# Gated delta rule plus mixture of experts on one core: decay exponents made on GpSimd instead of TensorE, and a reordered VectorE and GpSimd programme

## The chip, the cores and the metric

One core of a Trainium2 chip (trn2). The metric is the device time of one execution in microseconds. Engine names follow the profile: PE is TensorE, DVE is VectorE, ACT is ScalarE, POOL is GpSimd, SP is SyncE, whose queue here only issues DMAs.

## The reference, cut to what matters

```python
# x: (2, 2048, 256), 16 heads of 64
q, k, v = causal_dwconv(x @ Wq.T), causal_dwconv(x @ Wk.T), causal_dwconv(x @ Wv.T)   # 4 taps and a bias
g, beta = log_sigmoid(x @ Wg.T), sigmoid(x @ Wb.T)
k = k / clip(norm(k), 1e-12);  q = q * 64 ** -0.5
# per head, over time:
#   S = exp(g_t) * S + beta_t * (k_t v_t^T - k_t (S^T k_t)^T);   o_t = S^T q_t
x = layernorm(x + o @ Wo.T)
x = layernorm(x + shared_expert(x) + top6_of_64_experts(x))
```

## The kernel before, in words

The kernel has three phases. `gates_phase` computes the gates and, for all chunks of 64 tokens, the running sums of g inside a chunk. It stores these sums as rows in DRAM (`g_rows`) and their exponentials in `eg_rows`. `delta_phase` runs the recurrence in chunks. `ffn_phase` is the output projection, the layer norms and the experts; the change does not touch it.

`delta_phase` works on 64 macros. A macro is 256 tokens of both batches for one pair of heads, that is 16 units of 64 tokens in a 128x512 layout: 8 blocks of 64 columns (C = 64), and 64 partitions for each of two halves. A loop over `SLOTS` = 71 slots is written out for every engine, and each engine runs its own list of steps in order, tied to the others by semaphores. In slot t the macro m = t is projected (`project`, three outputs k, v, q through the single PSUM bank `p_j`), the macro `before` = t - 1 goes through keys, values, Gram products and mask, the macro `mi` = t - 5 has its triangular inverse completed (`inverse_r` to `horner`), and two steps of the state chain run (`chain_step`, called `one` and `two_`). Every second slot starts a group of two macros whose 16x16 diagonal blocks are inverted by forward substitution in 15 rows (`substitute`, L628 and L631, two small DVE operations per row on the tiles `xi`, `kb` and `outer`).

A causal convolution of four taps is done in this way: ACT writes the last tap with the bias (`last_tap`), DVE adds taps 2, 1 and 0 with `scalar_tensor_tensor` (`conv`, L574) for k and q. For v it adds taps 2 and 1 (`conv_values`, L588), and PE the rest.

The decay matrix of a macro, exp(cum_query - cum_key) with the later keys masked, is made in `exponents` (L417): one fp32 matmul over 82 partitions in which selector rows pick the row of sums and subtract the other, into `p_j`. ACT takes the exponential out of `p_j` into `ex` (`decay`, L730). POOL multiplies it by beta over the key length (`weight`, L876), and DVE uses it in `mask` (L617), which is nearly the last DVE step of a slot. The operands of that matmul are `arg_l` and `arg_r`: constants loaded once, and the rows of the macro loaded from `g_rows` by three small DMAs (`load_rows`, L269 and L271).

Other names: `residual` L646, `gate` L598 (keys and queries times `eg`), `update` L654, `lengths` L605, `inverse_lengths` L609, `horner` L638 on DVE; `decay_state` L888, `off_diagonal` L858, `carry_in` L844, `carry_out` L851, the copy of the identity into `xi` L908, `clip` L863, `factors` L869 and L870, `roots` L882 (a power of 128x8 elements) on POOL. The SP queue in a slot: `load_blocks` L299, `load_rows`, `load_decays` L279, `load_weights` L288, `load_inverse` L316 and L321, `store_o` L330, `store_inverse` L307.

Which operands lie in PSUM matters below. `residual`, `update`, `horner` and `mask` read one operand from PSUM (`p_c`, `p_i`, `p_xy`). `conv`, `conv_values`, `gate` and both operations of `substitute` read two tensors from SBUF.

Of the kernel before, what the change touches and what calls it, by code (L numbers as in the profile page):

```python
# [7 lines left out]
ALU = mybir.AluOpType  # L8
# [26 lines left out]
C_ID, C_INCL, C_SUF, C_ONES, C_SAME, C_SWAP, C_OFF, C_EYE, C_STRICT, C_REST, C_END = (  # L35
    0, 128, 256, 384, 512, 640, 768, 832, 1088, 1216, 1344)
# [16 lines left out]
def gates_phase(nc, a, s):  # L53

    sem = s.sem
    with ExitStack() as own:
# [15 lines left out]
        rows_out, cleared, args_in = sem("g_rows_out"), sem("g_cleared"), sem("g_args_in")  # L72
# [6 lines left out]
        def _(sp):  # L79
# [6 lines left out]
            for i in range(2):  # L86
                sp.dma_start(s.arg_l[i][:, :], a["arg_l"]).then_inc(args_in, 16)
                sp.dma_start(s.arg_r[i][:, :], a["arg_r"]).then_inc(args_in, 16)
            sp.wait_ge(args_in, 64)
# [23 lines left out]
        def _(pe):  # L113
# [19 lines left out]
            for k in range(4):  # L133
                pe.transpose(p_row[:, k * 128:k * 128 + 128], za[:, k * 128:k * 128 + 128],
                             s.const[:, C_ID:C_ID + 128]).then_inc(sums, 1)

        @block.vector
        def _(ve):
# [12 lines left out]
            ve.tensor_copy(za[:, 0:512], p_cum[:, :]).then_inc(dve, 1)  # L151
# [36 lines left out]
def delta_phase(nc, a, s):  # L188
# [5 lines left out]
    with ExitStack() as own:  # L194
# [15 lines left out]
        eg, ex, arg_l, arg_r = two("eg", 520), s.ex, s.arg_l, s.arg_r  # L210
# [51 lines left out]
        def _(sp):  # L262
            def load_rows(m):

                e = m % 2
                if m >= 2:
                    sp.wait_ge(exped, m - 1)
                for sh in range(2):
                    sp.dma_start(view(arg_l[e], sh * C, (1, C), parts=(64 + sh * 8, 8)),  # L269
                                 bass.AP(s.g_rows, m * 1024 + sh * 512, [[C, 8], [1, C]])).then_inc(r_in[e], 16)  # L270
                sp.dma_start(view(arg_r[e], 0, (1, 512), parts=(80, 2)),  # L271
                             bass.AP(s.g_rows, m * 1024, [[512, 2], [1, 512]])).then_inc(r_in[e], 16)
# [61 lines left out]
            load_tokens(0)  # L334
            load_weights(1)
# [23 lines left out]
        def _(pe):  # L359
            def project(m, n, done):  # L360
                e = m % 2
                if n == 1 and m == 0:
                    pe.wait_ge(tap_k, 1)
                if n == 1 and m >= 1:
                    pe.wait_ge(exped, m)
# [156 lines left out]
            for t in range(SLOTS):  # L522
# [13 lines left out]
                if is_macro(before):  # L536
                    exponents(before)
                if is_macro(before):
# [23 lines left out]
        def _(ve):  # L562
            def conv(m, i, tapped, done, taps=(2, 1, 0)):
# [3 lines left out]
                for tap in taps:  # L567
# [9 lines left out]
            def conv_values(m):  # L577
# [3 lines left out]
                for tap in (2, 1):  # L581
                    if tap == 2:
                        ve.wait_ge(tap_v, m + 1)
                        ve.wait_ge(carried, m + 1)
                    else:
                        ve.wait_ge(conv_v, 2 * m + 1)
                    column = (m % NPAIR * 3 + 2) * (TAPS + 1) + tap
# [984 lines left out]
```

## Time and profile before

| | |
|---|---|
| median of 3 runs | 1839.95 us (1837.96 to 1852.81) |
| the profiled execution | 1854.48 us, its span 1852.7 us |
| busy in the span | PE 1576.1, DVE 1201.7, ACT 890.0, POOL 863.5 us |
| slots of the delta phase | from about 60 to about 1200 us |

Times in the rows are microseconds from the span's start. The profiled execution is 0.8% above the median, so a difference worked out from the profile is added to the median.

### The profile page before, as it was taken

What the parts mean: (1) busy time and instruction counts of PE and PEld (TensorE: products, weight loads), DVE (VectorE), ACT (ScalarE), POOL (GpSimd) and SP (SyncE); (2) the same over time, 40 slices, a digit from 0 to 9 for tenths busy, and PEclk for the clock granted to TensorE, in tenths of its full rate; (3) what the DMA queues carried; (4) which work ended last, traced back from release to release, by engine and by line L of the source; (5) the groups of instructions that cost most, each with busy time, mean ns of one, the idle gap of its engine ahead of it and who ended that gap; (6) DMA issues with size and microseconds to landing.
All of it is one profiled execution on the core that took longest, in us unless ns stands there. A gap on an engine that the chain in (4) does not pass through costs nothing. (4 is left out here: it accounts for less than half of the span.)

```text
span 1852.7 us, 73957 instructions
## 1 busy us (share of the span) xinstructions
PE 1576.1 (85%) x31244; PEld 1175.0 (63%) x31244; DVE 1201.7 (65%) x3061; ACT 890.0 (48%) x2282; POOL 863.5 (47%) x1070
## 2 busy tenths in 40 slices
PE   7478999999899999999999997667888985898990
PEld 6235666666666666666666665556777874787870
DVE  1388988888889889888888886234445553222224
ACT  1276767767767767667667664100011110133333
POOL 0034444443444444434444443116655665577775
PEclk9799999999999999999999998887889997999995
DMA  6235564565555655655656554274444420499757
GB/s 269 82 83 115 114 133 114 124 128 116 123 126 114 138 113 123 135 114 113 137 114 126 111 117 99 56 240 118 140 130 133 138 80 27 110 259 248 166 88 284
DMA packets 521402, 245.45 MB, mean 132 GB/s; under 512 B 423888, under 2 KB 485968, under 8 KB 520176
## 3 DMA queue, kind: packets, MB, share of 16 engines
q1 hardware_dynamic: 368976, 200.72, 41.2%
q10 hardware_dynamic: 133632, 20.98, 6.1%
q0 software_dynamic: 18464, 19.03, 5.8%
q8 instruction: 247, 4.05, 0.9%
q14 instruction: 83, 0.68, 0.1%
HBM read 169.29 MB, written 71.37 MB: 130 GB/s over the span
## 5 line engine op out<-in xcount | busy, mean ns | idle before, releaser
L375 PE MATMUL delta_p_j<-delta_xt,delta_w 128*128 128x512 f32 x768 | 387.7, 628 | 30.5 <-DMA delta_xt<-in_xt 17.5
L574 DVE SCALAR_TENSOR_TENSOR delta_kq<-delta_hist,cw,delta_kq 128x512 f32<-128x512 f32 x384 | 298.6, 778 | 30.7 <-ACT delta_kq L722 23.7
L1395 POOL DMA_INDIRECT slot_tokens<-mix_tokens,mix_slot x192 | 188.5, 982 | 115.5 <-DVE mix_slot L1266 59.8
L715 ACT ACTIVATE delta_hist<-delta_p_j 128x512 f32<-128x512 f32 x192 | 114.8, 598 | 240.6 <-PE delta_p_j L375 233.4
L375 PEld LDWEIGHTS delta_p_j<-delta_xt,delta_w 128*128 128x128 f32 x768 | 132.0, 192 | 146.3 <-issue 111.8
L888 POOL TENSOR_TENSOR delta_sd<-state,eg_end 128x256 f32<-128x256 f32 x128 | 104.4, 816 | 258.2 <-DVE state L654 258.2
L1074 PE MATMUL mix_p_y<-mix_wo,mix_ot 128*128 128x256 f32 x512 | 134.3, 407 | 33.3 <-issue 15.6
L863 POOL TENSOR_SCALAR delta_n<-delta_n 128x8 f32<-128x8 f32 x64 | 15.5, 242 | 287.3 <-DVE delta_n L605 287.3
L1165 PE MATMUL mix_p_h<-mix_wo,w 128*88 128x128 f32 x1024 | 126.2, 277 | 13.5 <-ACT mix_wo L1351 10.4
L588 DVE SCALAR_TENSOR_TENSOR delta_yv<-delta_hist,cw,delta_yv 128x512 f32<-128x512 f32 x128 | 132.1, 1032 | 8.2 <-ACT delta_yv L722 5.9
L1074 PEld LDWEIGHTS mix_p_y<-mix_wo,mix_ot 128*128 128x128 f32 x512 | 99.3, 202 | 58.3 <-issue 44.9
L778 ACT ACTIVATE delta_kpv<-delta_kpv,delta_root 128x64 f32<-128x64 f32 x512 | 135.3, 344 | 0.0
L1165 PEld LDWEIGHTS mix_p_h<-mix_wo,w 128*88 128x88 f32 x1024 | 115.8, 158 | 29.8 <-ACT mix_wo L1351 22.8
L882 POOL TENSOR_TENSOR delta_root<-delta_n,half_power 128x8 f32<-128x8 f32 x64 | 133.9, 2093 | 0.0
L436 PEld LDWEIGHTS delta_p_i<-delta_kkq,rt 64*32 64x32 f32 (+1 forms) x4096 | 67.3, 100 | 105.1 <-DVE delta_kkq L638 98.2
L495 PEld LDWEIGHTS delta_p_c<-delta_r,delta_kkq 64*64 64x64 f32 x2048 | 70.8, 136 | 93.6 <-issue 86.9
L772 ACT ACTIVATE delta_kpv<-delta_kpv,delta_fk 128x64 f32<-128x64 f32 x512 | 128.8, 343 | 0.1
L1301 DVE SCALAR_TENSOR_TENSOR mix_wo<-mix_wo,mix_p_h 88x256 f32<-88x256 f32 x64 | 26.7, 417 | 147.9 <-ACT mix_wo L1357 118.7
L1418 POOL DMA_INDIRECT acc<-mix_ot,mix_places x64 | 100.6, 1572 | 45.1 <-ACT mix_ot L1363 27.3
L436 PE MATMUL delta_p_i<-delta_kkq,rt 64*32 64x32 f32 (+1 forms) x4096 | 81.3, 184 | 44.4 <-DVE delta_kkq L638 43.6
L646 DVE TENSOR_TENSOR delta_r<-delta_kpv,delta_p_c 128x256 f32<-128x256 f32 x128 | 53.3, 416 | 87.4 <-PE delta_p_c L470 86.9
L631 DVE TENSOR_TENSOR delta_xi<-delta_xi,delta_outer 128x15 f32<-128x15 f32 (+7 forms) x480 | 99.0, 206 | 16.5
(148 smaller groups left out, 3607.5 us busy)
## 6 DMA issues: line engine op xcount, KB each, us to landing
delta_xd<-x_scratch SPq DMA_DIRECT2D x256, 128.0 KB
delta_w<-in_wqkv SPq DMA_DIRECT2D x64, 416.0 KB
w<-in_w SPq DMA_DIRECT2D x64, 352.0 KB
delta_eg<-eg_rows SPq DMA_DIRECT2D x128, 130.0 KB, 3.2
n_scratch<-delta_kkq ACTq DMA_DIRECT2D x128, 128.0 KB
ot<-delta_o SPq DMA_DIRECT2D x128, 128.0 KB
mix_ot<-ot SPq DMA_DIRECT2D x16, 1024.0 KB
w<-in_w SPq DMA_DIRECT2D x64, 176.0 KB
```

The lines of the kernel that those rows point to most:

```text
L375: mm = pe.matmul(p_j[:, :], w[e][:, (ch * 3 + n) * 128:(ch * 3 + n) * 128 + 128], xt[m // 8 % 2][:, ch * 512:ch * 512 + 512], start=ch == ...
L436: mm = pe.matmul(view(p_i, g * C + first, (1, count), parts=(64 * sh, rows)), view(lhs, g * C, (1, rows), parts=half(sh)), view(rhs, at + ...
L574: ve.scalar_tensor_tensor(out, view(hist[e], i * 2 * 518 + tap, (259, 2), (1, 256)), cw[:, column:column + 1], out, ALU.mult, ALU.add).the ...
L588: ve.scalar_tensor_tensor(out, view(hist[e], 518 + tap, (259, 2), (1, 256)), cw[:, column:column + 1], out, ALU.mult, ALU.add).then_inc(co ...
L715: ac.activation(view(hist[e], n * 518 + 3, (259, 2), (1, 256)), p_j[:, :], ACT.Copy)
L772: ac.activation(kpv[:, at:at + C], kpv[:, at:at + C], ACT.Copy, scale=fk[:, g:g + 1]).then_inc(kp_out, 1)
L778: ac.activation(kpv[:, at:at + C], kpv[:, at:at + C], ACT.Copy, scale=root[:, g:g + 1]).then_inc(vp_out, 1)
L882: po.tensor_tensor(root[:, :], n2[:, :], view(s.half_power, 0, (0, 8)), ALU.pow).then_inc(small, 1)
L888: po.tensor_tensor(view(sd, 0, (128, 2), (C, 2), (1, C)), view(state, first_pair(group) * 128, (C, 2), (128, 2), (1, C)), view(s.eg_end, g ...
L1074: mm = pe.matmul(p_y[i % 2][:, 0:D], ot[i // 2 % 2][:, p * 256 + i % 2 * 128:p * 256 + i % 2 * 128 + 128], wo[:, p * D:p * D + D], start=p ...
L1165: mm = pe.matmul(p_h[e % 2][0:HALF, piece * 128:piece * 128 + 128], s.w13[:, at * 704 + ch * SI + piece * HALF:at * 704 + ch * SI + piece ...
L1395: po.indirect_dma_start(out=s.tok.ap(), out_offset=bass.IndirectOffsetOnAxis(ap=slot[i % 2][:, k:k + 1], axis=0), in_=tokens[:, i:i + 1], ...
```

## The change

The matmul of the exponents, its constants and its three small loads go. Two loads of 64 partitions by 2 KB put the row of sums, repeated over the partitions, into a tile `span`; they are issued one slot ahead. POOL subtracts the sums of the keys and adds the mask, in two operations in place, and ACT takes the exponential from `span`. The identity comes into `xi` by a DMA instead of a POOL copy. On DVE, tap 1 of the values moves to the start of the next slot, the keys' taps are no longer split, and the substitution rows are divided 8 (odd slots) and 7 (even slots) instead of 6 and 9. On POOL, `roots` moves ahead of `factors` and `weight`, and three waits on convolution semaphores are new.

```diff
             def load_rows(m):
...
                 for sh in range(2):
-                    sp.dma_start(view(arg_l[e], sh * C, (1, C), parts=(64 + sh * 8, 8)),
-                                 bass.AP(s.g_rows, m * 1024 + sh * 512, [[C, 8], [1, C]])).then_inc(r_in[e], 16)
-                sp.dma_start(view(arg_r[e], 0, (1, 512), parts=(80, 2)),
-                             bass.AP(s.g_rows, m * 1024, [[512, 2], [1, 512]])).then_inc(r_in[e], 16)
+                    sp.dma_start(span[e][64 * sh:64 * sh + 64, :],
+                                 bass.AP(s.g_rows, m * 1024 + sh * 512, [[0, C], [1, 512]])).then_inc(r_in[e], 16)
...
                 sp.wait_ge(kk_out[group % 2], 64 * (group // 2 + 1))
+                if group >= 1:
+                    sp.wait_ge(x_out[(group - 1) % 2], 16 * ((group - 1) // 2 + 1))
+                    sp.wait_ge(xit_out, group)
+                sp.dma_start(xi[:, :], a["const"][:, C_EYE:C_EYE + SUB * SUB]).then_inc(xi_set, 16)
...
                 if is_macro(t):
-                    load_rows(t)
                     load_decays(t)
                 if t % 8 == 2 and t // 8 + 1 < NSPAN:
                     load_tokens(t // 8 + 1)
+                if is_macro(t + 1):
+                    load_rows(t + 1)
...
-                if n == 1 and m == 0:
-                    pe.wait_ge(tap_k, 1)
-                if n == 1 and m >= 1:
-                    pe.wait_ge(exped, m)
+                if n == 1:
+                    pe.wait_ge(tap_k, m + 1)
...
-            def exponents(m):
-
-                e = m % 2
-                pe.wait_ge(r_in[e], 48 * (m // 2 + 1))
-                if m + 1 < NM:
-                    pe.wait_ge(tap_k, m + 2)
-                else:
-                    pe.wait_ge(tap_q, NM)
-                pe.matmul(p_j[:, :], view(arg_l[e], 0, (1, 128), parts=(0, 82)), view(arg_r[e], 0, (1, 512), parts=(0, 82)),
-                          start=True, stop=True).then_inc(arg, 1)
...
                 if is_macro(before):
+                    conv_values(before, 1)
                     conv(before, 1, tap_q, conv_q)
                     gate(before)
-                if even:
-                    substitute(subst_group, range(6, 9))
                 if one:
                     update(*one)
-                if is_macro(m):
-                    conv(m, 0, tap_k, conv_k, (2,))
+                if even:
+                    substitute(subst_group, range(8, 11))
+                if is_macro(m) and t % 2:
+                    conv(m, 0, tap_k, conv_k)
                 if two_:
                     residual(*two_)
-                if is_macro(m):
-                    conv(m, 0, tap_k, conv_k, (1, 0))
                 if even:
-                    substitute(subst_group, range(9, 11))
+                    substitute(subst_group, range(11, SUB - 1))
+                if is_macro(m) and t % 2 == 0:
+                    conv(m, 0, tap_k, conv_k)
                 if odd:
                     substitute(subst_group, range(0, 2))
                 if is_macro(before):
                     lengths(before)
-                if even:
-                    substitute(subst_group, range(11, SUB - 1))
                 if odd:
-                    substitute(subst_group, range(2, 6))
+                    substitute(subst_group, range(2, 4))
                 if is_macro(before):
                     inverse_lengths(before)
                 if is_macro(mi):
                     horner(mi, rx_done, 16, y1_out)
+                if odd:
+                    substitute(subst_group, range(4, 8))
                 if two_:
                     update(*two_)
-                if is_macro(m):
-                    conv_values(m)
+                if is_macro(m) and t % 2 == 0:
+                    conv_values(m, 2)
                 if is_macro(mi):
                     horner(mi, ry1_done, 32, y2_out)
+                if is_macro(m) and t % 2:
+                    conv_values(m, 2)
                 if is_macro(before):
                     mask(before)
...
+            def exponent(m):
+                e = m % 2
+                po.wait_ge(r_in[e], 32 * (m // 2 + 1))
+                po.tensor_tensor(view(span[e], 0, (C, 8), (1, C)), view(span[e], 0, (C, 8), (1, C)),
+                                 view(s.cum, m * 8, (1, 8), (0, C)), ALU.subtract).then_inc(arg, 1)
+                po.wait_ge(arg, 2 * m + 1)
+                po.tensor_tensor(view(span[e], 0, (C, 8), (1, C)), view(span[e], 0, (C, 8), (1, C)),
+                                 view(const, C_LATER, (0, 8), (1, C)), ALU.add).then_inc(arg, 1)
...
+                if is_macro(before):
+                    po.wait_ge(conv_v, 2 * before + 1)
                 if one:
                     decay_state(*one)
...
-                if t % 2 and 0 <= (t - 3) // 2 < NG:
...
-                    po.tensor_copy(xi[:, :], const[:, C_EYE:C_EYE + SUB * SUB]).then_inc(xi_set, 1)
+                if is_macro(m):
+                    if m >= 1:
+                        po.wait_ge(conv_q, 3 * m)
+                    exponent(m)
+                    po.wait_ge(conv_k, 3 * m + 3)
                 if two_:
                     decay_state(*two_)
                 if is_macro(before):
                     clip(before)
+                    roots(before)
                     factors(before)
                     weight(before)
-                    roots(before)
```

In the gates phase the four loads of `arg_l` and `arg_r` go, and the sums of the keys stay in SBUF as `cum`.

## Rows read from the trace of the kernel before

**Rows 1.** The view by stages: busy time of each engine in two stretches, then clock and DMA

```profile
core 0: us, PE busy (x) PEld busy (x) DVE busy (x) ACT busy (x) POOL busy (x), PEclk, DMA share, GB/s
400.00:600.00 200.00, 188.21 (x5095) 127.11 (x5093) 174.07 (x404) 138.99 (x351) 86.35 (x124) 1.00 0.57 123
...
1100.00:1200.00 100.00, 75.37 (x2465) 60.53 (x2465) 53.69 (x151) 39.00 (x103) 28.78 (x42) 0.88 0.42 84
```

**Rows 2.** The view of waits from 330 to 1000 us: total, times, longest

```profile
DVE delta_r L646 <- PE delta_p_c L470: 48.3, 39, 3.3
...
PE delta_p_i L436 <- DMA delta_xd<-x_scratch: 5.4, 6, 1.6
...
DVE delta_outer L628 <- DMA delta_kb<-n_scratch: 0.6, 2, 0.3
```

**Rows 3.** The view of line L617, from 330 to 1000 us

```profile
L617 DVE TENSOR_TENSOR delta_kkq<-delta_p_xy,ex x40: 1215/1217/1226, 330.2 to 989.3; 128x1024 f32<-128x1024 f32 x40
```

**Rows 4.** The timeline of DVE over one odd slot: start, duration, line, idle before

```profile
600.75 1.22 DVE L617 TENSOR_TENSOR delta_kkq<-delta_p_xy,ex 128x1024 f32<-128x1024 f32 x1
...
605.12 1.22 DVE L598 TENSOR_TENSOR delta_kqg<-delta_kq,delta_eg 128x1024 f32<-128x1024 f32 x1 [0.20 <-DVE delta_kq L574]
...
609.90 0.42 DVE L646 TENSOR_TENSOR delta_r<-delta_kpv,delta_p_c 128x256 f32<-128x256 f32 x1 [2.56 <-PE delta_p_c L470]
...
615.72 2.14 DVE L588 SCALAR_TENSOR_TENSOR delta_yv<-delta_hist,cw,delta_yv 128x512 f32<-128x512 f32 x2
...
618.11 1.22 DVE L617 TENSOR_TENSOR delta_kkq<-delta_p_xy,ex 128x1024 f32<-128x1024 f32 x1
```

**Rows 5.** The timeline of DVE over the even slot that follows

```profile
623.62 0.22 DVE L628 TENSOR_TENSOR delta_outer<-delta_xi,delta_kb 128x63 f32<-128x63 f32 x1
...
624.65 0.23 DVE L628 TENSOR_TENSOR delta_outer<-delta_xi,delta_kb 128x63 f32<-128x63 f32 x1
...
625.38 0.74 DVE L574 SCALAR_TENSOR_TENSOR delta_kq<-delta_hist,cw,delta_kq 128x512 f32<-128x512 f32 x1
...
628.95 0.68 DVE L605 TENSOR_REDUCE delta_n<-delta_sq 128x8 f32<-128x512 f32 x1
629.55 0.20 DVE L628 TENSOR_TENSOR delta_outer<-delta_xi,delta_kb 128x48 f32<-128x48 f32 x1
...
631.24 0.19 DVE L609 RECIPROCAL delta_rn<-delta_n 128x8 f32<-128x8 f32 x1
...
634.49 1.22 DVE L617 TENSOR_TENSOR delta_kkq<-delta_p_xy,ex 128x1024 f32<-128x1024 f32 x1
```

**Rows 6.** The timeline of POOL over the same two slots

```profile
615.48 1.04 POOL L876 TENSOR_TENSOR ex<-ex,delta_bp 128x512 f32<-128x512 f32 x1
616.48 2.11 POOL L882 TENSOR_TENSOR delta_root<-delta_n,half_power 128x8 f32<-128x8 f32 x1
618.57 0.62 POOL L888 TENSOR_TENSOR delta_sd<-state,eg_end 128x256 f32<-128x256 f32 x1
619.15 1.01 POOL L858 TENSOR_TENSOR noff<-delta_kkq,const 128x384 f32<-128x384 f32 x1
...
625.54 1.06 POOL L888 TENSOR_TENSOR delta_sd<-state,eg_end 128x256 f32<-128x256 f32 x1 [4.65 <-DVE state L654]
629.72 0.24 POOL L863 TENSOR_SCALAR delta_n<-delta_n 128x8 f32<-128x8 f32 x1 [3.12 <-DVE delta_n L605]
631.52 0.21 POOL L869 TENSOR_TENSOR delta_bp<-beta,delta_rn 128x8 f32<-128x8 f32 x1 [1.55 <-DVE delta_rn L609]
```

**Rows 7.** The timeline of DVE in the last microseconds, a tensor_tensor with two SBUF inputs

```profile
1827.58 1.19 DVE L1311 TENSOR_TENSOR w<-w 128x1024 f32<-128x1024 f32 x1
```

**Rows 8.** The timeline of POOL at the same place

```profile
1827.75 1.11 POOL L1437 TENSOR_SCALAR mix_crstd<-mix_cmv 128x4 f32<-128x4 f32 x1 [1.36 <-DVE mix_cmv L1317]
...
1831.74 0.23 POOL L1437 TENSOR_SCALAR mix_crstd<-mix_cmv 128x4 f32<-128x4 f32 x1
```

**Rows 9.** The timeline of PE in the odd slot: the matmul of the exponents

```profile
605.93 1.13 PE L417 MATMUL delta_p_j<-arg_r,arg_l 82*128 82x512 f32 x2
```

**Rows 10.** The timeline of the SP queue in the odd slot: DMA issues

```profile
606.00 1.50 SPq L299 DMA_DIRECT2D delta_kb<-n_scratch  x1
...
609.40 2.04 SPq L279 DMA_DIRECT2D delta_eg<-eg_rows  x2
```

More of the change, by code:

```diff
@@ L33 @@
 BIG = 3e38
-C_ID, C_INCL, C_SUF, C_ONES, C_SAME, C_SWAP, C_OFF, C_EYE, C_STRICT, C_REST, C_END = (
-    0, 128, 256, 384, 512, 640, 768, 832, 1088, 1216, 1344)
+C_ID, C_INCL, C_SUF, C_ONES, C_SAME, C_SWAP, C_OFF, C_EYE, C_STRICT, C_REST, C_LATER, C_END = (
+    0, 128, 256, 384, 512, 640, 768, 832, 1088, 1216, 1344, 1408)
 def view(t, offset, *dims, parts=None):
@@ L71, in gates_phase @@
         x_in = [sem(f"g_x_in{j}") for j in range(NSPAN)]
-        rows_out, cleared, args_in = sem("g_rows_out"), sem("g_cleared"), sem("g_args_in")
+        rows_out, cleared = sem("g_rows_out"), sem("g_cleared")
         logits, sums = sem("g_logits"), sem("g_sums")
@@ L85, in _ @@
                     sp.dma_start(s.cw[:, :], a["cw"]).then_inc(const_in, 16)
[L86 to L89, printed above, removed]
             sp.wait_ge(pool, 1)
@@ L150, in _ @@
             ve.wait_ge(sums, 1)
-            ve.tensor_copy(za[:, 0:512], p_cum[:, :]).then_inc(dve, 1)
+            ve.tensor_copy(s.cum[:, :], p_cum[:, :]).then_inc(dve, 1)
             ve.wait_ge(sums, 2)
@@ L209, in delta_phase @@
         yv = two("yv", 512)
-        eg, ex, arg_l, arg_r = two("eg", 520), s.ex, s.arg_l, s.arg_r
+        eg, ex, span = two("eg", 520), s.ex, two("span", 512)
         kpv, kkq, kqg = sb("kpv", 8 * 1024), sb("kkq", 8 * 1024), sb("kqg", 8 * 1024)
@@ L334, in _ @@
             load_tokens(0)
+            load_rows(0)
             load_weights(1)
@@ L536, in _ @@
                 if is_macro(before):
-                    exponents(before)
-                if is_macro(before):
                     turn_values(before, (2, 3))
@@ L562, in _, with conv @@
         def _(ve):
-            def conv(m, i, tapped, done, taps=(2, 1, 0)):
+            def conv(m, i, tapped, done):
                 e = m % 2
                 out = view(kq[e], i * 512, (256, 2), (1, 256))
-                for tap in taps:
+                for tap in (2, 1, 0):
                     if tap == 2:
@@ L575, in conv, with conv_values @@
                                             cw[:, column:column + 1], out, ALU.mult, ALU.add).then_inc(done, 1)
-            def conv_values(m):
+            def conv_values(m, tap):
                 e = m % 2
                 out = view(yv[e], 0, (256, 2), (1, 256))
[L581 to L587, printed above, removed]
-                    ve.scalar_tensor_tensor(out, view(hist[e], 518 + tap, (259, 2), (1, 256)),
-                                            cw[:, column:column + 1], out, ALU.mult, ALU.add).then_inc(conv_v, 1)
+                if tap == 2:
+                    ve.wait_ge(tap_v, m + 1)
+                    ve.wait_ge(carried, m + 1)
+                else:
+                    ve.wait_ge(conv_v, 2 * m + 1)
+                column = (m % NPAIR * 3 + 2) * (TAPS + 1) + tap
+                ve.scalar_tensor_tensor(out, view(hist[e], 518 + tap, (259, 2), (1, 256)),
+                                        cw[:, column:column + 1], out, ALU.mult, ALU.add).then_inc(conv_v, 1)
             def gate(m):
@@ L624, in substitute @@
                         ve.wait_ge(kb_in, 16 * (group + 1))
-                        ve.wait_ge(xi_set, group + 1)
+                        ve.wait_ge(xi_set, 16 * (group + 1))
                     else:
@@ L726, in decay @@
                 e = m % 2
-                ac.wait_ge(arg, m + 1)
+                ac.wait_ge(arg, 2 * m + 2)
                 if m >= 2:
                     ac.wait_ge(masked, m - 1)
-                ac.activation(view(ex[e], 1, (C + 1, 8), (1, C)), view(p_j, 0, (C, 8), (1, C)), ACT.Exp).then_inc(exped, 1)
+                ac.activation(view(ex[e], 1, (C + 1, 8), (1, C)), view(span[e], 0, (C, 8), (1, C)), ACT.Exp).then_inc(exped, 1)
             def keys_values(m):
@@ L879, in roots @@
             def roots(m):
+                po.wait_ge(clipped, m + 1)
                 if m >= 1:
@@ L1471, in program @@
             s.beta, s.kd, s.eg_end, s.noff, s.rt = (asb(n, 512) for n in ("beta", "kd", "eg_end", "noff", "rt"))
-            s.arg_l, s.arg_r = [asb(f"arg_l{i}", 128) for i in range(2)], [asb(f"arg_r{i}", 512) for i in range(2)]
+            s.cum = asb("cum", 512)
             s.cw, s.state, s.carry = asb("cw", NPAIR * 3 * (TAPS + 1)), asb("state", 1024), asb("carry", NPAIR * 18)
@@ L1498, in constants @@
     c[:, C_REST:C_REST + 128] = i >= j
+    c[:, C_LATER:C_LATER + C] = np.where(i[:, :C] % C <= j[:, :C], 0, NEG)
     return c
-def exponent_operands():
-    import numpy as np
-    left, right = np.zeros((128, 128), np.float32), np.zeros((128, 512), np.float32)
-    key, query = np.indices((C, C))
-    for n in range(8):
-        right[0:C, n * C:n * C + C] = np.where(key <= query, 0, NEG)
-        for sh in range(2):
-            right[64 + sh * 8 + n, n * C:n * C + C] = -1
-    for sh in range(2):
-        left[0:C, sh * C:sh * C + C] = np.eye(C)
-        left[80 + sh, sh * C:sh * C + C] = 1
-    return left, right
 def kernel(**inputs):
```

9 lines of the change are left out of this document (1 added, 8 removed).

## The prediction

> **What bounds the kernel now.** I read the stages first. Between 400 and 600 us PE is busy for 188 of 200 us and DVE for 174, at full clock [rows 1], so both look full, and only the order inside a slot tells which one sets the pace. The view of waits says it: DVE's largest wait is `residual` for the first matmul of the chain, 48.3 us in 39 cases, one every slot but unequal [rows 2]. The timelines show where it lies. In the odd slot, which runs from the end of one mask at 601.97 to the end of the next at 619.33 (17.36 us), DVE stands 2.56 us before L646 [rows 4]. The even slot, to 635.71, takes 16.38 us [rows 4, 5] and DVE stands almost nowhere in it: it is the bound there. Forty masks from 330.2 to 989.3 make 16.90 us a slot, 33.8 a pair [rows 3]. So the bound is DVE's list of steps, plus one PE wait in every second slot. POOL has time (86 of 200 us), but I read its rows for another thing: whom it delays.
>
> **How POOL and DVE delay each other.** `weight` (L876) runs from 615.48 to 616.52. L588 starts at 615.72 and its two operations take 2.14 us [rows 4, 6], where two of the length of L574 (0.74, the same form) and a gap would take about 1.53 [rows 5]. So the first was held until POOL had ended, all but 0.19 us of its start: 0.80 of overlap cost 0.61. The other way round, `decay_state` takes 0.62 us alone and 1.06 when it starts under an L574, and ends 0.48 us after it [rows 5, 6]. The engine that comes second waits. This isn't so for every pair. `mask` keeps its 1.22 us under L888 and L858, and its second operand comes from PSUM [rows 4, 6]; the second L588 ran at its own speed under `roots`, 2.11 us long [rows 4, 6]. Is it a matter of L574's form or of two inputs in SBUF? At the end of the kernel a plain tensor_tensor with two SBUF inputs (L1311, 1827.58 to 1828.77) holds up a 0.23 us POOL operation to 1.11 us, which ends 0.09 after it [rows 7, 8]. So I take it that two SBUF inputs decide, and `gate` and `substitute` have them. Before, no large POOL operation lay beside either of them in these slots; after, some do. That is the heart of this forecast.
>
> The Trainium skill says the same of the pair (SBUF — State Buffer, section Who interferes with whom): a VectorE instruction with two SBUF inputs contends with a GpSimd one that reads SBUF, and the later one blocks fully. The trace agrees where L588 waits for `weight`, all but 0.19 us; for a tensor_tensor that comes second no row shows it.
>
> **The change, part by part.**
>
> *PE.* The exponents' matmul goes, 1.13 us a slot ahead of `inverse_r` and the chain [rows 9]. That takes away 1.1 of the 2.56 us. The rest goes because DVE itself comes later to the second `residual` in the odd slot: tap 1 of the values (0.79 with its gap) and two more taps of the keys (1.57) now lie before it. Together 3.5 us against 2.56: the wait goes whole, and the next thing late is DVE. What could keep it is the load of `xd` on which `inverse_r` waits already, 5.4 us in 6 of some 20 odd slots [rows 2]; the substitution ends earlier by 1.7 us of rows (below), so its store and reload go out earlier, and I cost it at nothing.
>
> *SP.* Three loads go and two of 64 descriptors come, each much like an L279, which took 2.04 for two [rows 10]; they are needed a slot later and land under its work. Cost nothing. The identity's load stands ahead of `kb` (L299, 1.50 us [rows 10]), and `kb` was nearly late before, 0.6 us in two waits [rows 2]; DVE asks for it about a microsecond sooner. Between 0 and 0.5 us in the odd slot; I take 0, since the `xd` loads ahead of it in the queue go earlier too.
>
> *POOL, new.* Two operations of 128x512. The nearest rows are L876 (1.04, same form as the subtraction) and L858, 1.01 for 384 columns with the constant, which makes 1.35 for 512 [rows 6]. I take 1.04 and 1.2 (1.04 to 1.35 for the second). They are released by the end of the queries' taps, as is `gate`, which comes 0.20 us after it [rows 4]; POOL answers DVE in about 0.09 to 0.15 (L863 begins 0.09 after L605 [rows 5, 6]). So POOL is first by some 0.05 us, `gate` waits 1.04 - 0.05 - 0.19 = 0.8 us. The second POOL operation then waits for `gate` and ends 1.06 us after it. `update` (0.41, PSUM) runs beside it, and the next two-input operation is held: substitution row 8 in even slots, 0.7; the first tap of the keys in odd slots, 0.55 with its free start of 0.19. If `gate` gets in first, the sum is about the same, since three operations stand in one line either way.
>
> *Even slot, then.* `lengths` ended at 10.30 in the slot. Before it come now tap 1 (+0.79) and rows 11 to 14 (+1.7, from 629.55 to 631.24), and rows 6 and 7 are gone (-1.03, 623.62 to 624.65) [rows 5]: 11.76. With 0.8 and 0.7 it is 13.3. After `lengths` POOL must do in order: answer 0.09, `clip` 0.24, an answer to itself 0.1 (my estimate from the 0.09), `roots` 2.11, `factors` 0.35, `weight` 1.04, and an answer of 0.1, before `mask` 1.22 [rows 5, 6]. That is 5.25 us. DVE's own rest (`inverse_lengths`, `horner`, `update`, one L588, `horner`) is only 2.1 to 2.4 us. So `mask` now waits for `weight`, because `roots` stands in front of it and because `lengths` comes late. End of slot 18.5 against 16.38.
>
> *Odd slot.* From 17.36: the wait -2.56; the hold of L588 under `weight` gone, tap 1 moved with its gap, -0.57 in all; rows 6 and 7 in, +1.03; `gate` +0.8; taps +0.55; `decay_state` (0.62), now released by the keys' taps, beside the first substitution row, +0.35; `weight`, now beside rows 4 to 7, between 0 and 1.04, I take 0.6. Sum 17.56. Here `roots` costs nothing, as `lengths` comes earlier.
>
> Pair 36.1 against 33.8: +2.3 us. Thirty pairs (64 slots, the first few without chain work) give +69. The gates phase and the experts I leave unchanged: the four loads that go ended far ahead of their users. On the profiled run that is 1923.5, on the median 1909.
>
> **The rivals.**
>
> *A tensor_tensor is not held* (only L574 and L588 are). Then the even slot is 18.5 - 1.5 = 17.0 and the odd one 17.56 - 0.8 - 0.35 - 0.6 = 15.8; 32.8 a pair, -30 us: 1810. For it: no row shows a tensor_tensor made to wait. Against: L1311. Chance 0.1.
>
> *The hold is partial*: POOL lets DVE in for part of its operations, or the small substitution steps slip through, or `roots` overlaps more than in line. Half the holds, 36.1 - 1.6 = 34.5: +21, to 1861; with less still, no change within 1%. Chance of a result from 1822 to 1858: 0.12; of 1858 to 1876: 0.06.
>
> *Everything late at once*: `kb` +0.5, `weight` its full 1.04, the second operation 1.35 in both slots: +1.2 a pair more, 1945. A second way there: PE's share falls from 94% to about 83%, and where it was 75% the granted clock was 0.88 of full, so partly 1.2 GHz [rows 1]. PE's waits would stay under 2 us each, so I don't expect it. Above 1938 together 0.08.
>
> *`roots` holds DVE too.* By the skill's page (SBUF — State Buffer, section SBUF: two separate sides) the pair is held for the whole GpSimd instruction. As a mechanism here: in odd slots `roots` lies beside rows 2 to 7 and would hold DVE for up to 2.11 us, 38.2 a pair, 1972. The second L588 at full speed under L882 speaks against it [rows 4, 6]. Chance 0.03, inside the 0.08.
>
> **How the numbers follow.** Forecast: holds as computed, 1876 to 1938, chance 0.62. Its ends: 1.2 a pair if both open odd terms are 0 and the second operation is 1.04 (+36), and nearly 3.3 if most are at their upper ends. One per cent is about what a measurement of this kernel tells from no change. Range 1842 to 1938: it takes in the forecast, the partial holds and the upper half of "no change" (0.06), 0.74, and what of the worst case lies just at its edge, near 0.8. Faster by over 1%: 0.12 (the first rival 0.1, and 0.02 for the partial one at its best); within 1%: 0.12; slower: 0.76.
>
> **What would show each step.** L598's mean over 1.9 us, not 1.22; the first L628 of even slots (128x63) long, with others unchanged; L876 as the last releaser of L617 in even slots, with some 2 us of DVE idle; no wait of L646 on L470; the two new POOL operations at 1.04 and 1.0 to 1.35 unless they start under a `gate`; even slots longer than odd ones. Wrong would be: L598 at 1.22 beside a POOL operation (first rival); L628 waiting for `kb`; PE waiting for `xd` longer than now.

## The result and the profile after

The changed kernel takes 1905.7 us (median of 4 runs, 1904.27 to 1906.87) against 1839.98 us for the one before on the same chip: ratio 1.0338 [1.0306, 1.037], +65.7 us (the two medians alone give 1.036, inside the interval). Its profiled execution took 1906.42 us, span 1904.6. That is +51.9 on the profiled execution of before, which lay some 14 us above its own median; the profiles don't show to which stage those 14 us belong.

The lost time lies in the delta phase. From the end of the first mask to the end of the last it takes 1106.0 us, before 1051.3 (+54.8). Below, "even" and "odd" give the mean of 20 slots of each kind (slots 22 to 61), from mask to mask, and "pair" their sum. Which 40 slots are taken moves a pair by 0.05 to 0.15 us in both kernels and by up to 0.35 in some of the experiments. Before: 16.49 + 17.32 = 33.82. After: 17.76 + 17.82 = 35.57. The +1.75 in some 31 pairs is the +54.

The view by windows (columns: length; busy us and instructions of PE, PE's weight loads, DVE, ACT, POOL; granted clock; DMA share; GB/s) is the one to set beside [rows 1]:

```profile
400.00:600.00 200.00, 171.34 (x4902) 119.20 (x4895) 179.69 (x381) 131.43 (x339) 102.85 (x136) 0.98 0.60 133
```

PE fell from 188 to 171 us: it waits more and has less to do. DVE rose from 174 to 180 us though it ran fewer instructions (381, before 404). So its instructions got longer. Line numbers are those of each kernel's own file, so a step has another number than in the kernel before. The groups by form, 340 to 1040 us, name them (columns: count, busy us, mean ns, idle before and its releaser):

```profile
L559 DVE SCALAR_TENSOR_TENSOR delta_kq<-delta_hist,cw,delta_kq 128x512 f32<-128x512 f32 x237 | 191.3, 807 | 5.6
L582 DVE TENSOR_TENSOR delta_kqg<-delta_kq,delta_eg 128x1024 f32<-128x1024 f32 x39 | 77.8, 1994 | 8.2 <-DVE delta_kq L559 7.1 <-PE delta_p_c L494 1.2
L601 DVE TENSOR_TENSOR delta_kkq<-delta_p_xy,ex 128x1024 f32<-128x1024 f32 x39 | 47.6, 1221 | 24.4 <-PE delta_p_xy L414 24.4
...
L638 DVE TENSOR_TENSOR state<-delta_sd,delta_p_c 128x256 f32<-128x256 f32 x79 | 32.5, 411 | 0.0
...
L854 POOL TENSOR_TENSOR delta_span<-delta_span,const 128x512 f32<-128x512 f32 x39 | 83.4, 2138 | 3.1
L879 POOL TENSOR_TENSOR delta_root<-delta_n,half_power 128x8 f32<-128x8 f32 x40 | 67.2, 1680 | 3.4
...
L851 POOL TENSOR_TENSOR delta_span<-delta_span,cum 128x512 f32<-128x512 f32 x39 | 40.7, 1044 | 103.1 <-DVE delta_kq L559 103.1
```

`gate` is now L582: 1994 ns in the mean, 1.22 before. `mask` (L601) and `update` (L638) kept their lengths; both read PSUM. POOL's second new operation (L854) reads 2138, because each one starts under a `gate`. DVE's one large idle time is before `mask` (24.4 us in 20 cases, one an even slot). `residual` (L630) has no wait left in this window, where before it had 48.3 us from 330 to 1000 us [rows 2].

An odd slot and the even one behind it, in the timeline of DVE (start, length):

```profile
600.49 2.00 DVE L582 TENSOR_TENSOR delta_kqg<-delta_kq,delta_eg 128x1024 f32<-128x1024 f32 x1 [0.20 <-DVE delta_kq L559]
602.41 0.41 DVE L638 TENSOR_TENSOR state<-delta_sd,delta_p_c 128x256 f32<-128x256 f32 x1
602.74 3.01 DVE L559 SCALAR_TENSOR_TENSOR delta_kq<-delta_hist,cw,delta_kq 128x512 f32<-128x512 f32 x3
...
606.00 0.48 DVE L612 TENSOR_TENSOR delta_outer<-delta_xi,delta_kb 128x15 f32<-128x15 f32 x1
...
608.34 0.21 DVE L615 TENSOR_TENSOR delta_xi<-delta_xi,delta_outer 128x48 f32<-128x48 f32 x1
...
610.20 1.11 DVE L612 TENSOR_TENSOR delta_outer<-delta_xi,delta_kb 128x63 f32<-128x63 f32 x1
...
613.33 1.22 DVE L601 TENSOR_TENSOR delta_kkq<-delta_p_xy,ex 128x1024 f32<-128x1024 f32 x1
...
615.69 2.31 DVE L559 SCALAR_TENSOR_TENSOR delta_kq<-delta_hist,cw,delta_kq 128x512 f32<-128x512 f32 x3
618.20 2.00 DVE L582 TENSOR_TENSOR delta_kqg<-delta_kq,delta_eg 128x1024 f32<-128x1024 f32 x1 [0.20 <-DVE delta_kq L559]
...
620.46 0.96 DVE L612 TENSOR_TENSOR delta_outer<-delta_xi,delta_kb 128x63 f32<-128x63 f32 x1
...
626.88 0.68 DVE L589 TENSOR_REDUCE delta_n<-delta_sq 128x8 f32<-128x512 f32 x1
627.92 0.20 DVE L593 RECIPROCAL delta_rn<-delta_n 128x8 f32<-128x8 f32 x1 [0.36 <-POOL delta_n L859]
...
631.09 1.23 DVE L601 TENSOR_TENSOR delta_kkq<-delta_p_xy,ex 128x1024 f32<-128x1024 f32 x1 [1.22 <-PE delta_p_xy L414]
```

And POOL beside it:

```profile
600.37 1.04 POOL L851 TENSOR_TENSOR delta_span<-delta_span,cum 128x512 f32<-128x512 f32 x1 [3.01 <-DVE delta_kq L559]
601.49 2.14 POOL L854 TENSOR_TENSOR delta_span<-delta_span,const 128x512 f32<-128x512 f32 x1
605.83 0.62 POOL L885 TENSOR_TENSOR delta_sd<-state,eg_end 128x256 f32<-128x256 f32 x1 [2.20 <-DVE delta_kq L559]
...
608.14 1.69 POOL L879 TENSOR_TENSOR delta_root<-delta_n,half_power 128x8 f32<-128x8 f32 x1
...
610.19 1.04 POOL L872 TENSOR_TENSOR ex<-ex,delta_bp 128x512 f32<-128x512 f32 x1
...
619.21 2.13 POOL L854 TENSOR_TENSOR delta_span<-delta_span,const 128x512 f32<-128x512 f32 x1
...
627.97 1.67 POOL L879 TENSOR_TENSOR delta_root<-delta_n,half_power 128x8 f32<-128x8 f32 x1
...
629.95 1.04 POOL L872 TENSOR_TENSOR ex<-ex,delta_bp 128x512 f32<-128x512 f32 x1
```

Read them line against line. L851 starts 0.12 us ahead of `gate` and ends at 601.41; `gate` ends at 602.49, 1.08 later. L854 waits for `gate` and ends at 603.63. `update` slips through beside it in 0.41 us. The keys' taps behind it take 3.01 instead of 2.31, and in the even slot the first substitution row takes 0.96 instead of 0.22. `weight` (L872) turns one row at 610.20 into 1.11 us. Under L879 the rows keep their 0.2 us.

At the end of the even slot DVE stands 1.22 us before `mask`. The profile names PE's L414:

```profile
629.22 1.10 PE L414 MATMUL delta_p_xy<-delta_kq 64*64 64x128 f32 x32
```

It ended at 630.32. `weight` ended at 630.99, and `mask` began 0.10 us behind that. So the releaser was POOL, whose chain runs from `lengths` (ended 627.56) through `clip`, `roots`, `factors` and `weight`. Two experiments below test this reading.

### The profile page after: what moved, and what is told of

It is laid out like the page before. It is cut to its first block and busy times, and to the rows that moved or that the text cites. A ratio compares the mean times of both kernels' runs of the same rounds, so it can differ in the third digit from the quotient of the medians.

```text
span 1904.6 us, 73944 instructions
## 1 busy us (share of the span) xinstructions
PE 1525.4 (80%) x31116; PEld 1163.6 (61%) x31116; DVE 1282.3 (67%) x3061; ACT 880.0 (46%) x2282; POOL 976.3 (51%) x1166
## 5 line engine op out<-in xcount | busy, mean ns | idle before, releaser
L373 PE MATMUL delta_p_j<-delta_xt,delta_w 128*128 128x512 f32 x768 | 400.6, 646 | 39.4 <-DMA delta_xt<-in_xt 17.6
L559 DVE SCALAR_TENSOR_TENSOR delta_kq<-delta_hist,cw,delta_kq 128x512 f32<-128x512 f32 x384 | 311.7, 812 | 34.6 <-ACT delta_kq L709 25.5
L885 POOL TENSOR_TENSOR delta_sd<-state,eg_end 128x256 f32<-128x256 f32 x128 | 79.7, 623 | 337.7 <-DVE delta_kq L559 223.4
L851 POOL TENSOR_TENSOR delta_span<-delta_span,cum 128x512 f32<-128x512 f32 x64 | 66.8, 1044 | 176.6 <-DVE delta_kq L559 170.5
L1072 PE MATMUL mix_p_y<-mix_wo,mix_ot 128*128 128x256 f32 x512 | 126.9, 397 | 27.3 <-DMA mix_wo<-in_wo 15.1
L612 DVE TENSOR_TENSOR delta_outer<-delta_xi,delta_kb 128x15 f32<-128x15 f32 (+7 forms) x480 | 130.5, 272 | 20.9 <-DMA delta_kb<-n_scratch 9.7
L854 POOL TENSOR_TENSOR delta_span<-delta_span,const 128x512 f32<-128x512 f32 x64 | 135.9, 2124 | 5.0
L582 DVE TENSOR_TENSOR delta_kqg<-delta_kq,delta_eg 128x1024 f32<-128x1024 f32 x64 | 127.3, 1989 | 13.1 <-DVE delta_kq L559 10.8
L615 DVE TENSOR_TENSOR delta_xi<-delta_xi,delta_outer 128x15 f32<-128x15 f32 (+7 forms) x480 | 120.9, 252 | 16.5
```

The costliest lines, as they stand in the source:

```text
L373: mm = pe.matmul(p_j[:, :], w[e][:, (ch * 3 + n) * 128:(ch * 3 + n) * 128 + 128], xt[m // 8 % 2][:, ch * 512:ch * 512 + 512], start=ch == ...
L559: ve.scalar_tensor_tensor(out, view(hist[e], i * 2 * 518 + tap, (259, 2), (1, 256)), cw[:, column:column + 1], out, ALU.mult, ALU.add).the ...
L582: ve.tensor_tensor(view(kqg, ring(m), (512, 2), (C, 8), (1, C)), view(kq[e], 0, (512, 2), (C, 8), (1, C)), view(eg[e], 0, (1, 2), (C + 1, ...
L612: ve.tensor_tensor(view(outer, 0, (left, i), (1, left)), view(xi, row, (SUB, i), (0, left)), view(kb, row * SUB + row + 1, (0, i), (1, lef ...
L615: ve.tensor_tensor(view(xi, row + 1, (SUB, i), (1, left)), view(xi, row + 1, (SUB, i), (1, left)), view(outer, 0, (left, i), (1, left)), A ...
L854: po.tensor_tensor(view(span[e], 0, (C, 8), (1, C)), view(span[e], 0, (C, 8), (1, C)), view(const, C_LATER, (0, 8), (1, C)), ALU.add).then ...
```

## The experiments

Ratios below are to the kernel before on the same chip. Theory: the two POOL operations and DVE's two-input ones stand in one line, and `roots` with a late `lengths` makes the even slot wait. Rivals: the two larger loads or the traffic cost the time; the new places of the steps do, wherever the exponents are made; PE does (`mask` <- L414). e_pe_exp, e_one_op, e_after_gate and e_roots_last ran on a chip where the kernel before took only 1766.69 us: their stretch behind the last mask is 623 to 626 us, where the kernel before has 711 in its profile. The delta phase is not faster there: e_pe_exp took 1041.0 us from first to last mask on this chip and 1040.7 on another. So pairs can be compared over chips, and ratios nearly so (on the shorter total the same loss reads 1.038 where another chip shows 1.036).

**e_pe_exp: the exponents back on PE, all else of the change kept.**

```diff
                 if is_macro(before):
+                    exponents(before)
+                if is_macro(before):
                     turn_values(before, (2, 3))
...
-                    exponent(m)
...
-                if is_macro(t + 1):
-                    load_rows(t + 1)
```

> The changed kernel with the exponents back as the matmul of before, with its three small loads; everything else of the change stays (order of DVE and POOL, identity by DMA, roots ahead of weight). Theory of holds (a POOL operation and a DVE operation with two SBUF inputs run one after the other): gate falls from 1.99 to 1.22, the first substitution row of even slots and the first tap of the keys in odd slots to their own length, together 1.5 and 1.45 us a slot, so about 3.0 us of a pair of 35.6 and 31 pairs: 92 us less than the changed kernel, about 1814, and faster than before. Rival (the reordering or the early roots cost the time, the exponents on POOL don't): 1885 or more.

Ratio 0.9971 [0.9945, 0.9998]; pair 33.59 (16.51 + 17.07). Groups by form, then waits from 330 to 1000 us (total us, times, longest), of this kernel:

```profile
L601 DVE TENSOR_TENSOR delta_kqg<-delta_kq,delta_eg 128x1024 f32<-128x1024 f32 x42 | 51.5, 1225 | 8.8 <-DVE delta_kq L578 8.8
```

```profile
DVE delta_kkq L620 <- PE delta_p_xy L431: 24.3, 20, 1.2
DVE delta_outer L631 <- DMA delta_kb<-n_scratch: 21.0, 14, 3.4
```

`gate` is back at 1225 ns. The usual even slot is 16.25 us, which is 17.76 less the two holds of 0.77 and 0.74; it still has its wait of 1.2 us before `mask`. So the POOL exponents carry the whole loss, and the steps' new places, taken together, carry none of it. But the gain over before is 0.3% and not the 1.4% expected (1814 of 1840 us). The odd slot, 15.99 us at its shortest, waits for `kb` in 14 of 20 cases, 21.0 us in all. That is 1.05 us a pair, about what the pair of 33.59 lies above the 32.6 that the expected holds leave (35.57 less 2.95).

**e_before_loads: the kernel before, with the two larger loads added** (their tile is written and not read).

```diff
+                for sh in range(2):
+                    sp.dma_start(span[e][64 * sh:64 * sh + 64, :],
+                                 bass.AP(s.g_rows, m * 1024 + sh * 512, [[0, C], [1, 512]])).then_inc(span_in[e], 16)
...
```

> The kernel before with the two new loads of 128 KB a slot added, into a tile that nothing reads. If it is the traffic that costs (rival), 1.01 to 1.03. Theory of holds: they hide, 1.000 to 1.004.

0.9984 [0.9962, 1.0007], pair 33.88. The loads cost nothing that can be measured; that rival is gone.

**e_one_op: the subtraction left out**, so one POOL operation of 512 columns remains.

```diff
-                ac.wait_ge(arg, 2 * m + 2)
+                ac.wait_ge(arg, m + 1)
...
-                po.tensor_tensor(view(span[e], 0, (C, 8), (1, C)), view(span[e], 0, (C, 8), (1, C)),
-                                 view(s.cum, m * 8, (1, 8), (0, C)), ALU.subtract).then_inc(arg, 1)
-                po.wait_ge(arg, 2 * m + 1)
```

> The changed kernel without the subtraction of the keys' sums, so the decay matrix is wrong; one POOL operation is left in place of two. Theory of holds: gate is still held by about 0.8 or more (the length of the mask's addition, 1.04 to 1.35, less 0.24), but the second hold is gone (0.74 in even, 0.68 in odd slots): 1.4 a pair, 44 us less, 1862. Rival (it is POOL's load or the DMA traffic): 1900 or more.

1.021 [1.0171, 1.0249], pair 34.98 (17.23 + 17.74). Groups by form:

```profile
L582 DVE TENSOR_TENSOR delta_kqg<-delta_kq,delta_eg 128x1024 f32<-128x1024 f32 x40 | 88.9, 2223 | 8.5 <-DVE delta_kq L559 8.3 <-PE delta_p_c L494 0.2
...
L851 POOL TENSOR_TENSOR delta_span<-delta_span,const 128x512 f32<-128x512 f32 x40 | 50.8, 1271 | 105.3 <-DVE delta_kq L559 105.3
```

The mask's addition by itself takes 1.27 us, and `gate` behind it 2.22. The longer POOL operation holds it longer: 1.27 against 1.04 gives +0.23, and so it came out. By slots: even +0.23 - 0.74 = -0.51 (measured -0.53); odd +0.23 - 0.70, and `kb` late by 13.0 us in all instead of 5.5 (+0.37 a pair), -0.10 (measured -0.08). The gain over the changed kernel is under half of the expected one (0.59 of 1.4 us a pair; ratio 1.021, with 1862 us or 1.012 expected and 1.033 the rival's): the longer hold of `gate` and the load of `kb` took back 0.83 us a pair.

**e_after_gate: the exponents released by `gate`** instead of the queries' taps, so that POOL comes second.

```diff
-                        po.wait_ge(conv_q, 3 * m)
+                        po.wait_ge(gated, m)
```

> The changed kernel with the exponents released by gate instead of by the queries' taps. gate runs at 1.22; the two POOL operations then hold the next two-input operations of DVE twice, 1.8 against 1.5 in even slots and about 1.5 against 1.45 in odd ones: the same within 1%, 1906 to 1917. Rival (only the collision with gate matters): 24 us faster per 0.8 of a slot, about 1857.

1.0379 [1.0348, 1.041], pair 35.80 (18.06 + 17.74). Groups by form:

```profile
L582 DVE TENSOR_TENSOR delta_kqg<-delta_kq,delta_eg 128x1024 f32<-128x1024 f32 x39 | 47.8, 1225 | 8.2 <-DVE delta_kq L559 7.2 <-PE delta_p_c L494 1.0
...
L615 DVE TENSOR_TENSOR delta_xi<-delta_xi,delta_outer 128x63 f32<-128x63 f32 x38 | 40.0, 1051 | 1.3
...
L612 DVE TENSOR_TENSOR delta_outer<-delta_xi,delta_kb 128x63 f32<-128x63 f32 x38 | 25.3, 665 | 0.7
```

`gate` is free at 1225 ns, and the steps behind it pay: L615 takes 1051 ns in the mean instead of 540. The line is no shorter, only its order has changed; the even slot is even 0.3 us longer, as forecast (1.8 against 1.5). Moving the release doesn't help.

**e_roots_last: `roots` behind `weight` again, as before.**

```diff
                     clip(before)
-                    roots(before)
                     factors(before)
                     weight(before)
+                    roots(before)
```

> The changed kernel with roots after weight, as before the change. The pure chain on POOL gets 1.67 shorter and mask in even slots waits 1.2 us less (rival: 37 us faster, 1869). Theory of holds: weight then lies at 14.0 to 15.05 in the even slot and holds L572 there, so that only 0.65 is won, and the later off_diagonal holds the first tap of the next slot by about as much: 1886 to 1906.

1.0271 [1.024, 1.0302], pair 35.21 (17.06 + 18.15). DVE has no wait before `mask` left in the whole stretch. PE's L414 stands where it stood: it ends at 15.77 us in the even slot here and in the changed kernel (mean of 20), and `mask` begins at 15.84 instead of 16.53. So PE didn't release it in the changed kernel. The even slot wins 0.7 and not the 1.22 of idle. DVE, POOL and PE in the timeline:

```profile
625.24 1.36 DVE L572 SCALAR_TENSOR_TENSOR delta_yv<-delta_hist,cw,delta_yv 128x512 f32<-128x512 f32 x1
...
626.85 1.21 DVE L601 TENSOR_TENSOR delta_kkq<-delta_p_xy,ex 128x1024 f32<-128x1024 f32 x1
...
625.01 1.05 POOL L872 TENSOR_TENSOR ex<-ex,delta_bp 128x512 f32<-128x512 f32 x1
626.01 2.12 POOL L879 TENSOR_TENSOR delta_root<-delta_n,half_power 128x8 f32<-128x8 f32 x1
...
625.67 1.10 PE L414 MATMUL delta_p_xy<-delta_kq 64*64 64x128 f32 x32
```

`weight` moved off the path and onto a `conv_values` step (1.36 instead of 0.74). The expectation puts the lost half microsecond down to that hold, but these rows show a second cap at the same place: L414 ends at 626.77, 0.08 us before `mask`. Without the hold, PE's products would have kept `mask` there; which of the two counts was not tested. The odd slot lost 0.33: `roots` now starts late and pushes `off_diagonal` (1003 ns in the changed kernel, here 1224 in the mean) under the keys' and queries' taps, whose mean is 867 ns instead of 807.

**e_order: `lengths` ahead of substitution rows 11 to 14** (even) **and 0 to 1** (odd).

```diff
-                if even:
-                    substitute(subst_group, range(11, SUB - 1))
                 if is_macro(m) and t % 2 == 0:
                     conv(m, 0, tap_k, conv_k)
+                if is_macro(before):
+                    lengths(before)
+                if even:
+                    substitute(subst_group, range(11, SUB - 1))
...
```

> The changed kernel with one move on DVE: in even slots the keys' taps and lengths come ahead of substitution rows 11 to 14, in odd slots lengths comes ahead of rows 0 and 1. Nothing is left out. Theory (in even slots mask waits for the line lengths, clip, roots, factors, weight on POOL): lengths ends 1.75 earlier there; weight then holds the last L572 by about 0.5, and the even slot falls from 17.76 to about 16.8; odd slots as they are: 31 to 34 us less than the changed kernel, ratio to the kernel before 1.015 to 1.018. Rival (mask waits for PE's products, whose end the wait is put down to): the products keep their place, since the wait ends with them, and nothing is won: 1.034.

1.0174 [1.0146, 1.0202], pair 34.83 (16.76 + 18.07). DVE and POOL in the timeline:

```profile
616.64 0.68 DVE L589 TENSOR_REDUCE delta_n<-delta_sq 128x8 f32<-128x512 f32 x1
...
619.87 1.44 DVE L572 SCALAR_TENSOR_TENSOR delta_yv<-delta_hist,cw,delta_yv 128x512 f32<-128x512 f32 x1
...
621.56 1.21 DVE L601 TENSOR_TENSOR delta_kkq<-delta_p_xy,ex 128x1024 f32<-128x1024 f32 x1
...
619.71 1.04 POOL L872 TENSOR_TENSOR ex<-ex,delta_bp 128x512 f32<-128x512 f32 x1
```

Only DVE's order was touched. The wait goes, the even slot wins 1.0 us, and `weight` makes L572 0.7 us longer, about as in the run before. PE's products did not quite keep their place: they end 0.39 us earlier in the even slot (15.38), but `mask` begins 0.98 earlier (15.55), which PE alone can't explain. It now begins 0.17 us behind them, so that they are the next thing in its way. The odd slot loses 0.25: `horner` waits for PE there (11.0 us in all, 2.5 in the changed kernel), and PE for the reload of `xd` (36.2 us in 19 cases, none in the changed kernel), which fits a substitution that ends later. Both runs say the same: the wait before `mask` was for POOL's chain. The change's own order with `lengths` moved is worth 1.6% of the 3.4% lost.

**e_pe_order: both, the exponents on PE and that order.**

```diff
+                    exponents(before)
...
-                    exponent(m)
...
+                if is_macro(before):
+                    lengths(before)
+                if even:
+                    substitute(subst_group, range(11, SUB - 1))
```

> The same move together with the exponents on PE (as in e_pe_exp, ratio 0.997). Theory: the even slot loses its 1.22 before mask less the hold of L572, 0.75 net, and in odd slots lengths fills 0.6 of the wait for the diagonal blocks: 1.35 a pair, 42 us, ratio 0.973. Rival (the load of the blocks moves with the mask and eats it): 0.985 or more.

0.9911 [0.9873, 0.9949], pair 33.21 (15.79 + 17.42): ahead of both kernels, but by a third of what was expected (0.9% for 2.7%; the pair lies 0.38 under that of e_pe_exp, with 1.35 expected). The ratio is in the rival's range, 0.985 or more. Its waits, 330 to 1000 us:

```profile
DVE delta_r L649 <- PE delta_p_c L474: 16.7, 22, 2.0
DVE delta_outer L631 <- DMA delta_kb<-n_scratch: 13.1, 14, 1.6
...
PE delta_p_i L440 <- DMA delta_xd<-x_scratch: 11.6, 12, 1.6
DVE delta_kkq L641 <- PE delta_p_i L440: 11.5, 14, 2.3
```

DVE's list alone is no longer the bound. Late now are the two trips through DRAM, `kb` for the substitution and `xd` behind it, and with `xd` the PE matmuls for which DVE waits.

**e_pe_best: e_pe_order with the identity's load issued ahead of the wait for the stores** that `kb` needs.

```diff
-                sp.wait_ge(kk_out[group % 2], 64 * (group // 2 + 1))
                 if group >= 1:
                     sp.wait_ge(x_out[(group - 1) % 2], 16 * ((group - 1) // 2 + 1))
                     sp.wait_ge(xit_out, group)
                 sp.dma_start(xi[:, :], a["const"][:, C_EYE:C_EYE + SUB * SUB]).then_inc(xi_set, 16)
+                sp.wait_ge(kk_out[group % 2], 64 * (group // 2 + 1))
```

> As e_pe_order, and the identity's load is issued before SP waits for the stored products, not between them and the load of the blocks. The blocks are issued about 0.4 earlier: 0.2 to 0.4 an odd slot, 6 to 12 us below e_pe_order, ratio 0.967 to 0.970.

0.991 [0.9879, 0.9942], pair 32.99. A miss: 0.967 to 0.970 was expected, and there is no gain over e_pe_order that can be measured. The wait for `kb` fell only from 13.1 to 10.1 us, 0.15 an odd slot. The 0.4 us between the two issues isn't the main part of what makes it late.

**Three runs on one other chip** ask what makes `kb` late: e_pe_exp again, e_pe_exp with the identity copied by POOL as before, and e_pe_exp with only 64 of the 832 weight columns loaded from the third macro on.

```diff
-                sp.dma_start(xi[:, :], a["const"][:, C_EYE:C_EYE + SUB * SUB]).then_inc(xi_set, 16)
...
+                    po.tensor_copy(xi[:, :], const[:, C_EYE:C_EYE + SUB * SUB]).then_inc(xi_set, 1)
```

```diff
-                sp.dma_start(w[e][:, :], a["wqkv"][m % NPAIR, :, :]).then_inc(w_in[e], 16)
+                cols = WCOLS if m < 2 else 64
+                sp.dma_start(w[e][:, 0:cols], a["wqkv"][m % NPAIR, :, 0:cols]).then_inc(w_in[e], 16)
```

> e_pe_exp once more, on the chip of the other two: 0.997 again, and the waits for the diagonal blocks as before (21.7 us).

> e_pe_exp with the identity copied into xi by POOL again, as before the change. e_pe_exp came out at 0.997 of the kernel before, where 0.95 to 0.96 was worked out from its holds alone, and in odd slots it waits about a microsecond for the diagonal blocks (kb). If the identity's load, issued just ahead of that of the blocks, is what makes it late: the wait goes, 0.980. If the blocks are late because the products that they are read from land late: within 0.005 of e_pe_exp.

> e_pe_exp with loads of 64 of 832 weight columns from the third macro on, so the projections use old weights: 384 of some 2,000 KB a slot less traffic, and the queue ahead of the blocks and of the inverse shorter. If the loads of a slot wait on one another in the queue (theory): the waits for kb fall to under half of 21.7 us and the odd slot nears 16.0 from 17.1, ratio 0.975 to 0.985. If the chain of stores and reloads is a matter of latency alone: as e_pe_exp.

In that order: 0.9989 [0.9964, 1.0015], 0.9946 [0.9918, 0.9975], 0.994 [0.9911, 0.9969]; pairs 33.38, 33.14, 33.36; waits for `kb` 15.5, 8.2 and 16.9 us. The first is the kernel whose earlier trace had 21.0: one kernel differs by 5.5 us between two traces. (Of the second expectation's numbers, 0.95 to 0.96 is a share of the changed kernel's time; of the kernel before it is 0.986.) Without the identity's load the wait is about half, 0.37 us an odd slot less, and the ratio lower by 0.004, not the 0.98 of "the wait goes". Taking the weights' traffic away (DMA share 0.59 to 0.51) leaves the wait within that spread: a queue full of other data isn't the main cause. In one slot of e_pe_exp the path is: two stores issued by ACT up to 1.33 us in the slot, the second landed at 5.77, identity issued 5.82, `kb` issued 6.21, landed 10.21. The stores' 4.4 us and the load's 4.0 are the size of it; in that slot DVE stood 2.48 us for `kb`. What sets these two stays open.

## Why the prediction was right

Forecast 1909 us, measured 1905.7, and by the mechanism named. By its steps:

*The line of POOL and DVE.* Right. A tensor_tensor with two SBUF inputs is held, all but a start: `gate` takes 1994 ns in the mean where I had 1.22 + 0.8. e_pe_exp and e_after_gate free it, e_one_op lengthens it with POOL's operation. The second operation then costs 0.74 in even slots (0.7 forecast) and 0.70 in odd ones (0.55). `mask` and `update`, with an operand in PSUM, kept their lengths. By the Trainium skill (SBUF — State Buffer, section Who interferes with whom) a VectorE instruction with two SBUF inputs contends with a GpSimd instruction that reads SBUF. The trace agrees for the case that no row of before showed, a tensor_tensor that comes second: 1.99 against 1.22 us.

*PE's wait goes whole.* Right: no wait of `residual` is left from 340 to 1040 us.

*Loads at nothing, `kb` between 0 and 0.5.* Right in size: 5.5 us in 6 cases, 0.27 an odd slot, and e_before_loads shows the new loads free. DVE waiting for `kb` stood among the signs of being wrong, and it came, in that small size; PE waits for `xd` not longer but not at all. I had not seen that `kb` is the floor just under the present bound: the versions that took DVE's time away ran into it.

*POOL's new operations.* 1.04 as taken. The second is 1.27 by itself, with 1.2 forecast and 1.35 as the upper end.

*Even slot 18.5.* Measured 17.77 in the timeline. Here a size was off, by 0.73 us. `roots` was put at the 2.11 of [rows 6]; it takes 1.67. Before, it started under the first L588 (616.48, when that one, held by `weight`, ran to 617.07), and so its length held 0.44 us of waiting. It ended 1.53 us behind that step. e_roots_last, where it starts under L572, has 2.12 again and the same 1.53. The other 0.29 is `lengths`, which ended at 13.01 in the slot, not 13.3; 0.15 of it is a hold that is gone (see the odd slot). That `mask` waits for `weight` was right, by 1.22 us of idle and not the some 2 that I named as a sign.

*Odd slot 17.56.* Measured 17.82. In the timeline's slot `weight` beside the rows cost 0.89 with 0.6 taken (0 to 1.04), `decay_state` 0.31 with 0.35 (606.00: 0.48 instead of 0.17). Over the 20 odd slots the rows are held 0.97 us in the mean, as forecast (0.95). The tap (+0.15), `kb` (+0.27) and `gate` (0.77 for 0.8) make +0.4, and the slot is longer by 0.26 only. What I had not counted as won is a hold of the kernel before: `off_diagonal` (L858, 601.78 to 602.78) lay beside the first tap of the queries.

```profile
602.41 2.52 DVE L574 SCALAR_TENSOR_TENSOR delta_kq<-delta_hist,cw,delta_kq 128x512 f32<-128x512 f32 x3
```

Three free taps take 2.31 us (615.69 above). Over the 20 odd slots that first tap took 0.93 us before and 0.75 after, when tap 1 of the values stands ahead of it; in even slots 0.89 and 0.74. With this -0.18 the forecast's sum comes to 17.8.

*The sum.* +2.3 a pair was +1.75, and the profiled executions differ by 51.9 us where I had 69. The medians differ by 65.7, as the profiled execution of before lay 14 us above its median. That the forecast came within 4 us is in part luck: the mechanism's size was 0.55 a pair too large.

*Rivals.* "Not held" is excluded by `gate`: 38 of its 39 cases take 2.00 to 2.01 us and one takes 1.63. "Partial" is excluded for the same reason and because the small rows are held too (0.96 for 0.22); only `roots` cost less than in line. "All late" didn't come: `kb` +0.27, and a granted clock of 0.98 from 400 to 600 us, before 1.00. "`roots` holds DVE" didn't either, although a page of the Trainium skill (SBUF — State Buffer, section SBUF: two separate sides) would have the pair held for a whole GpSimd instruction. The trace differs: under L879 (608.14 to 609.83) the row at 608.34 keeps its 0.21 us. That the 128x8 power reads little and computes long would fit, but no run tested the reason.

## What to carry to other kernels

Work moved to GpSimd is not free time gained on another engine. In the rows read here, all but those of `roots`, a GpSimd operation that reads SBUF and a VectorE operation with two SBUF inputs stood in one line; what it lay beside for nothing were VectorE operations with a PSUM operand (`update` 0.41 us, `mask` 1.22). Before moving a step, take the durations of rows that ran undisturbed, and look one floor lower than the bound that you remove: here the usual even slot and the shortest odd slot of e_pe_exp make 16.25 + 15.99 = 32.24 us a pair, 1.6 under before, and a DRAM round trip of some 9 us kept its mean at 33.59.

## What the runs showed that was not expected

- The duration of a POOL instruction can hold its wait: `roots` 2.11 to 2.12 when it starts under a conv step, 1.67 otherwise; L854 2.14 under `gate`, 1.27 alone. `roots` waits for DVE, but does not hold DVE.
- A hold grows with the operation ahead: 1.04 gives `gate` +0.77, 1.27 gives +1.00. In both, 0.27 us of POOL's time costs `gate` nothing.
- The view of waits put 24.4 us of `mask`'s idle time down to PE. e_roots_last, with PE's matmul in its place and POOL's chain shorter, took the wait away. PE was not far, though: in e_roots_last and e_order `mask` begins 0.07 and 0.17 us behind PE's products, so a still shorter chain on POOL would win next to nothing there.
- One chip ran the stretch behind the last mask in 623 us, another in 713, for the same kernel (e_pe_exp and e_pe_exp_again) and the same length of the delta phase, 1041 us. Why is open.
